# The normalising product behind the sixth maximum, its low part behind the first mask

## What is computed

```
xn = layernorm(x)
q, k, v = xn @ Wq.T, xn @ Wk.T, xn @ Wv.T          # per head, rotary on q and k
scores = q @ k.T / sqrt(32), causal
attn = softmax(scores);  a = (attn @ v) @ Wo.T
top_vals, top_idx = top_k(xn @ gate_w.T, 2);  w = softmax(top_vals)
y = sum over the two of w * (xn @ expert_w[e].T + expert_b[e])
out = x + a + y
```

## Time and profile before

| | |
|---|---|
| median of three runs | 1005.22 us |
| profiled execution, device time | 1005.21 us |
| its span, first to last instruction | 1003.4 us |
| TensorE busy | 928.0 us (92%) |
| VectorE busy | 746.7 us (74%) |
| GpSimd busy | 565.2 us (56%) |
| ScalarE busy | 435.3 us (43%) |
| granted TensorE clock, mean over the span | 0.984 of full |
| multiplication into o_sb (L1501) in steps 17 to 27 | every 20.99 us, from 694.00 to 903.86 us |
| the same in steps 28, 29, 30, 31 | 924.84, 944.71, 963.17, 978.78 us |

### The profile page before, as it was taken

One profiled execution on the slowest core, in us unless ns is written; L12 is line 12 of the kernel. 1 busy time (PEld: TensorE's weight loads), 2 busy tenths in 40 slices (PEclk: granted clock), 3 DMA queues, 4 the chain that ended last, 5 costly groups with the idle time before them and its releaser, 6 DMA issues.

```text
span 1003.4 us, 18600 instructions
## 1 busy us (share of the span) xinstructions
PE 928.0 (92%) x6437; PEld 439.5 (44%) x6469; DVE 746.7 (74%) x1442; ACT 435.3 (43%) x711; POOL 565.2 (56%) x557
## 2 busy tenths in 40 slices
PE   2898989989999988989999999989999999999887
PEld 1344434434444533445555555543444444444333
DVE  7988987878889899554444444477878888788965
ACT  5367866756665432341211211214433444434442
POOL 1545575674666548562333333237887788777641
PEclk9999999999999999899999999999999999999999
DMA  6366588698787353286555555564555574455531
GB/s 238 115 212 231 140 277 301 198 297 297 197 263 265 117 200 96 79 348 196 177 171 176 178 169 172 169 217 138 189 154 169 161 235 149 145 171 170 181 107 54
DMA packets 107963, 188.62 MB, mean 188 GB/s; under 512 B 11872, under 2 KB 65248, under 8 KB 102624
## 3 DMA queue, kind: packets, MB, share of 16 engines
q1 hardware_dynamic: 97072, 152.03, 44.7%
q0 software_dynamic: 10800, 35.40, 12.7%
HBM read 117.13 MB, written 70.25 MB: 187 GB/s over the span
## 4 chain that ended last, share of the span: by engine, by line
PE 61%; DVE 16%; DMA 10%; POOL 5%; ACT 3%; issue 3%; SPq 2%; another core or an unknown queue 0%; DVEq 0%; ACTq 0%; POOLq 0%
PE psum L951 18%; PE psum L1039 7%; PE psum L1063 6%; PE psum L1002 5%; PE psum L1048 5%; PE psum L969 5%; PE psum L1005 5%; PE psum L989 4%; PE psum L928 4%; DMA x_in<-x 3%; DVE top L1480 3%; DMA xT_rows<-gT 2%; DVE den_turned L1496 1%; DVE rden L1498 1%; POOL k_hl L593 1%
## 5 line engine op out<-in xcount | busy, mean ns | idle before, releaser
L765 ACT ACTIVATE pT<-psum,factors 128x512 f32<-128x512 f32 (+1 forms) x352 | 219.7, 641 | 265.9 <-PE psum L989 256.1
L1039 PE MATMUL psum<-xT,w_att 128*128 128x512 f16 x768 | 198.7, 385 | 5.9 <-DVE xT L1426 4.7
L951 PE MATMUL psum<-w_exp,x_gT 128*128 x852 | 197.0, 381 | 0.7 <-DVE x_gT L1431 0.6
L1480 DVE TENSOR_REDUCE top<-psum 128x1 f32<-128x384 f32 (+3 forms) x232 | 141.7, 644 | 22.7 <-PE psum L972 19.1
L969 PE MATMUL psum<-k_stack,q_stack 96*128 96x384 f16 (+3 forms) x512 | 129.0, 305 | 26.7 <-DVE top L1480 18.9
L613 POOL DMA_INDIRECT x_g<-xn_rows,tok_of x71 | 67.3, 948 | 141.4 <-PE psum L928 134.6
L989 PE MATMUL psum<-q_stack,k_stack 98*128 98x256 f16 (+3 forms) x512 | 128.8, 305 | 7.0 <-ACT pT L765 6.0
L1431 DVE TENSOR_TENSOR x_gT<-psum,x_gT 128x512 f16<-128x512 f32 x71 | 49.0, 692 | 108.8 <-ACT x_gT L789 108.8
L951 PEld LDWEIGHTS psum<-w_exp,x_gT 128*128 128x128 f16 x852 | 83.8, 98 | 87.0 <-issue 3.3
L789 ACT ACTIVATE x_gT<-psum 128x512 f16<-128x512 f32 x71 | 42.3, 597 | 171.0 <-PE psum L928 171.0
L597 POOL TENSOR_SCALAR_AFFINE_SELECT pT<-pT 128x512 f32<-128x512 f32 x128 | 99.0, 784 | 19.6 <-ACT pT L765 19.4
(11 more groups left out here) (174 smaller groups left out, 1349.7 us busy)
## 6 DMA issues: line engine op xcount, KB each, us to landing
y_rows<-y_sb SPq DMA_DIRECT2D x71, 256.0 KB, 2.2
w_in<-w_all SPq DMA_DIRECT2D x12, 1024.0 KB, 10.0
q_stack<-qk_rows SPq DMA_DIRECT2D x96, 128.0 KB, 2.7
k_stack<-qk_rows SPq DMA_DIRECT2D x96, 128.0 KB, 2.9
x_in<-x SPq DMA_DIRECT2D x8, 1024.0 KB, 13.3
qk_rows<-q_hl SPq DMA_DIRECT2D x32, 256.0 KB, 2.2
qk_rows<-k_hl SPq DMA_DIRECT2D x32, 256.0 KB, 2.3
xn_rows<-x_in SPq DMA_DIRECT2D x8, 1024.0 KB, 4.8
```

Source lines behind the costliest of these rows:

```text
L765: act.activation(p_of(j, h, heads), banks[BANK_T + (NT_ * n + k) % 2][:, 0:W], ACT.Exp, scale=factors[:, 0:1]).then_inc(exp_done, 1)
L951: now = pe.matmul(banks[s % 4], x_gT[s % 4][:, xp * C + c, :], w_exp[:, bass.ds(e, 1), wp, c, :].rearrange("p e d -> p (e d)"), start=n == ...
L1039: now = pe.matmul(bank, w_att[:, what, wp, c, g * P:(g + 1) * P], xT[b % 2][:, xp * C + c, :], start=at_pass == 0, stop=at_pass == 3 * C - 1)
L1480: dve.tensor_reduce(out=top[:, h:h + heads, i], in_=of.rearrange("p (h t) -> p h t", h=heads), axis=AX.X, op=ALU.max)\
```

## The change

In steps 17 to 31 `normalise_o` is cut in two. `invert_sums` (wait, transposition, inversion, transposition) stays where it was on VectorE, behind maximum 3. The multiplication moves behind maxima 4 and 5, ahead of `rotate(0)`. In the same steps GpSimd's `low_o` moves from ahead of `rope(0)` to behind mask 0. Steps 0 to 15 and the call between them and the experts keep their order of instructions, and step 16 has neither operation.

```diff
                     gather_y(late_tiles(n + 1)[0])
-                if n >= 1 and n != N1:
+                if 1 <= n < N1:
                     low_o(n - 1)
                 if n + 3 < N:
                     rope(0, n + 3)
                 mask(n, 0)
+                if n > N1:
+                    low_o(n - 1)
                 if n + 3 < N:
                     low_qk(0, n + 3)
...
-            def normalise_o(n):
+            def invert_sums(n):
                 dve.wait_ge(pv_done, J * (n + 1))
...
                 own.link(dve.transpose(rden[:], rden_few[:].unsqueeze(2).broadcast_to([P, S // HD, HD])))
+
+            def normalise_o(n):
                 if n:
                     dve.wait_ge(o_lo, n)
                 dve.tensor_tensor(o_sb[:], banks[BANK_O], rden[:], ALU.mult).then_inc(o_read, 1)
...
                 if n and n != N1:
+                    invert_sums(n - 1)
+                if n and n < N1:
                     normalise_o(n - 1)
                 if n in KEEP_AT:
                     read_logits(KEEP_AT[n])
                 if nxt:
                     largest_score(n + 1, 4)
                     largest_score(n + 1, 5)
+
+                if n > N1:
+                    normalise_o(n - 1)
                 if ahead:
                     rotate(0, n + 3)
...
             low_xg(1)
+            invert_sums(N1 - 1)
             normalise_o(N1 - 1)
```

## The result

The changed kernel takes 1012.77 us (median of four runs, 1011.53 to 1014.92) where the kernel before takes 1003.14 us (median of four, 999.62 to 1005.86; one run has been added to those shown at the start). The ratio is 1.010, with a 95% interval of 1.0058 to 1.0143: the change costs about 1%. The forecast was 1009.9 us in a range of 1004.5 to 1013.5 us.

What follows compares the result with a forecast made beforehand. TensorE was taken as full (20.79 of 20.98 us in a regular step), so only its hold-ups count. Terms 1.0 + 1.1 + 1.0 + 1.6 = 4.7 us on 1005.2 gave 1009.9 us, range 1004.5 to 1013.5.

Steps and rivals of the forecast that it cites:

- Part 1: VectorE, regular steps: tile 6's 0.27 us wait goes, tile 8 waits 0.27 us longer for maximum 6; worth nothing.
- the sign that I gave: Regular steps: the weight loader's idle time before score tile 8 is near 0.7 us.
- The rival that the early maxima would be a gain: First rival: tile 8's wait does not grow, so steps 17 to 30 gain; 1003.6 us, chance 0.10.
- Part 3, regular steps: GpSimd, steps 17 to 27: mask 1 1.00 us late against 0.98 us of cover; 0.1 us a step, +1.1 us.
- the sign that mask 1's products follow mask 1 at once: Steps 17 to 27: TensorE's products with mask 1 start directly behind it, its 0.98 us of cover used up.
- Step 28: No value projection, so mask 1 sets TensorE's start without cover; +1.0 us, bounds 0.7 and 1.2.
- Steps 29 and 30: Late high_o delays exponential 2 and transposed tile 4; 0 to 0.9 us a step, 0.5 taken twice, +1.0 us.
- The third rival: TensorE's clock falls once more after new idle time in steps 28 and 31; 1011.2 to 1012.5 us, chance 0.14.
- Step 31: The projection waits longer for low_o(30), now behind mask 0; 1.2 to 2.1 us later, +1.6 us taken.
- The second rival: One more GpSimd collision with VectorE before mask 1 in each step, about 0.5 us each; 1015.4 us, chance 0.14.
- the fourth: Cover holds in regular steps and the end hides half of steps 28 to 31's 3.6 us; 1007.0 us, chance 0.12.

Runs made afterwards that it cites:

- kernels 5 and 6: Matmuls of no use keep TensorE busy in steps 29 and 30: 5 on the changed kernel (ratio 1.0025), 6 on the kernel before (0.9976).
- kernel 8: Kernel before plus useless matmuls in steps 29 and 30, and a new order with three-operation split in steps 17 to 28: 1007.43 us, ratio 0.9995.
- kernel 7: The changed kernel with the split's first two operations taking a constant instead of a second SBUF operand; ratio to the kernel before 1.0071.
- 10 and 11: Kernel before plus useless matmuls in steps 29 and 30 and a two-operation split (10: ratio 0.9956); 11 adds a new order in steps 17 to 27 (0.9912).
- kernel 2: The kernel before with only low_o moved behind mask 0, the multiplication staying ahead of maximum 4; ratio 1.0046.

## Why the prediction came out as it did

The direction was right and the measured time lies in the range, near its upper end; "slower" had been given 0.46, a little less than "no difference". The forecast said +4.7 us, the steps of the profile give +6.6 us, the medians +9.6 us. That the sum is not further off is in part luck: one term came out too large, one much too small, and one was right for a reason that did not hold. Term by term:

- **Part 1 (0 forecast).** Right. Tile 6's wait went, and tile 8's stayed: 5.35 us behind the transposition against 5.32. The expected bound of 0.05 us a step covered what came. Maximum 4 began at 820.52, 0.1 us behind the end of the linked transposition (819.70 + 0.71 = 820.41); its own score tile ended at 820.38, so it may be that tile that it now waits for, which no run tests. 0.03 us of it are left at tile 8. The loader's idle time before tile 8 did not grow to 0.7 us, the sign that I gave; it is 0.42 us, since its wait for the exponential (0.47 us, at 823.50) now lies just ahead. The rival that the early maxima would be a gain fell.
- **Part 3, regular steps (+1.1 forecast, +0.37 in the trace with part 1).** The cover of mask 1 was sized rightly, the delay was not. Mask 1 ends 13.94 us behind the transposition, before 13.46: 0.48 us later, not 1.00, as plain_k took 1.30 instead of 1.74 us. 0.54 us of cover are left, so the sign that mask 1's products follow mask 1 at once did not come. The collisions with VectorE went elsewhere, to the short operations of the split: two of them now take 1.17 and 1.30 us, where before one took 1.13. In a regular step that costs about 0.01 us: c's transposition stands 11.82 us behind the transposition of the sums, before 11.78 (829.92 - 818.14), and 0.03 of the difference were there at tile 8. The step that failed is that the split of the maxima did not stand in my list of what low_o's move passes: I looked at GpSimd's queue and who waits for it, and not at VectorE's short operations beside it.
- **Step 28 (+1.0 forecast, +0.96).** The size is right by luck, the named releaser is wrong: mask 1 was 0.47 us late, not 1.0, and had cover, and TensorE waited for the split (1.52 us of idle time before 935.57, before 0.41). Only when the split is shortened does mask 1 take its place, and then because plain_k collides again.
- **Steps 29 and 30 (+1.0 forecast, +3.49).** The mechanism is right and the term mis-sized. Transposed tile 4 starts 0.95 us later behind the transposition in step 29 (4.76 against 3.81), as I had worked out (0.9), but of that 0.70 us a step stay, not 0.5, by kernels 5 and 6. The rest, 2.1 us, is clock, which stood in this term at nothing. The third rival had the price of a slow stretch at 1.3 us, which came to about 1.0 (2.1 us for two more), but put it in steps 28 and 31; TensorE's clock stayed at 1.00 in step 28, and where the added waits met steps that already had one slow stretch, they got a second.
- **Step 31 (+1.6 forecast, +1.75).** Right: low_o ended at 988.78 us, 6.63 us behind the transposition, before at 4.93, and TensorE waited 1.56 us for it, where 1.6 were the sign.

The second rival (one collision more in each step, 1015.4 us) didn't come; the first (1003.6 us) fell with part 1. Of the fourth (1007.0 us) one half came, mask 1's cover held in the regular steps, and the other did not, since the end hid nothing. Why the medians differ by 2.7 us more than the profiles stays open. The untouched part before step 17 spreads by 8.6 us over the profiles, which is more than enough, and each median is of four executions, but no run here separates it.

## What to carry to other kernels

Moving an operation off one wait pays only if the next wait on the same queue doesn't follow: read two releases ahead, here from tile 6 to tile 8, before a wait is counted as gain. When a GpSimd operation is moved, list VectorE's short operations that then fall beside its row: such of 0.2 us became 1.2 us each, and joining three into two turned the new order of kernel 8 from 0.38 us lost in a regular step into 0.35 us gained. But read on to what VectorE does next: in step 28 a shorter split only moved the additions onto GpSimd's plain_k, and nearly nothing was left of the gain. And where TensorE waits several times in one stretch, price the waits and the slower matmuls behind them as one term; a few matmuls of no use in the wait can be the cheapest edit.

## What the runs showed of the hardware

- A 128x16 operation of VectorE that stands beside GpSimd's 128x512 ones lasts until GpSimd's operation is done, and ends 0.02 to 0.04 us behind it (step 23 of the changed kernel: the first ends at 829.00, GpSimd's at 828.97): 1.08 to 1.30 us in place of 0.16 to 0.23. That holds for two operands in SBUF and for one and a constant (kernel 7: 1.15 and 1.30 us in step 28; kernel 8: 1.20 us). It did not where GpSimd stood idle between two operations: at 830.25, between turned_k, which ended at 830.19, and plain_k, which started at 830.27, one took 0.17 us. The Trainium skill (SBUF — State Buffer, Who interferes with whom) names tensor_scalar among the operations that can contend with GpSimd when their operands meet certain conditions; in these rows it waited, and no run here shows which condition decides.
- In step 29 the clock was still full (granted 1.00) in 947 to 948 us and at 1.2 GHz (0.50) in 948.4 to 949 us, in the kernel before and in the changed one alike. Before, TensorE had waited 1.64 us until 945.99; in the changed kernel it had waited 1.04 us until 947.05 and was 0.2 us into the second wait, of 1.39 us, and the slow stretch behind that was twice as long. With these waits filled by matmuls the clock stayed at 2.4 GHz in both steps of kernels 5, 6, 8, 10 and 11. The same order of work on TensorE had one slow stretch in one step and two in the other (kernel 2), so their number isn't set by the order of work alone.
